# Adjacency and mixture-of-experts kernel on one core: z transposed through memory in 32 by 32 blocks, routing chain among the Q items, z's scaling one item later

## The chip, the cores and the metric

The kernel runs on one core of one Trainium2 chip. The metric is the device time in microseconds of one execution, lower is better. TensorE (PE in the profile) does the matmuls, VectorE (DVE) and ScalarE (ACT) the elementwise work, GpSimd (POOL) small statistics and one sum, and SyncE (SP) issues all transfers.

## The reference

```python
def _l0_gnn(x):                                  # on layernorm(x), x is (16, 512, 128)
    h = x @ fc_in_w.T + fc_in_b
    alph = sigmoid(alpha_train)[:, None]
    w_eff = w * clip(d, 0, 1) @ w.T
    for _ in range(8):                           # dt = 1/8
        f = alph * 0.5 * (adj @ h - h) + h @ w_eff - h + x
        h = h + dt * f
    return h

def _moe(tokens):                                # on layernorm(x), 8 experts, top 2
    probs = softmax(tokens @ router_w.T)
    rw, re = top_k(probs, 2); rw = rw / rw.sum(-1)
    out = tokens
    for e in range(8):
        out = out + combine[:, e:e + 1] * (gelu(tokens @ w1[e] + b1[e]) @ w2[e] + b2[e])
    return out

x = x + _l0_gnn(layernorm(x))
x = x + _moe(layernorm(x))
```

## The kernel before

The 16 batches are worked on in 8 groups of two (`GB = 2`). A group passes through two halves of a pipeline. In iteration `g`, the graph part of group `g` runs first and then the experts of group `g - 1`. Iteration 0 has no experts, iterations 1 to 6 are one loop body, and iteration 7 and the experts of group 7 are written out behind it. Every product is taken in three matmuls of a high and a low part (`mm3`, lines 1034 to 1036): ScalarE copies the high part (`high`, line 414), and VectorE subtracts it for the low part (`low`, line 605).

**Graph part.** The eight Euler steps are folded into a polynomial. TensorE multiplies the normalised input x0 with two powers of the nodes' matrix (`nodes_product(0)` to `(3)`, two for each of the two batches; their results become G, tile `GT`), then, in eight Q items of nine matmuls each, G by the features' powers `M` (line 1255); VectorE adds the bias to each item (line 957), and an item may not start before the sum of the one four back. Two stages of a Horner scheme with the nodes' matrix follow (`y1`, then `h8`), and the result is x1 (line 1000). Its statistics (line 609) go to GpSimd, which works out the inverse root in ten small operations (`inverse_root`, lines 366 to 387).

**Experts.** `experts(h, g, more)` runs 16 items for group `h`: item `i` is batch `i // 8`, expert `i % 8`. For an item TensorE does the up product (three matmuls of 512 columns), ScalarE the gelu (line 537), VectorE the scaling with the routing weight (line 902), ScalarE the high part, VectorE the low part, and TensorE, five items later (`LAG`), the down product (lines 1211 and 1218). From item 3 on an up product waits for the gelu of three items before. Among the items stand the steps for group `g`, which is one ahead: `scale_z` (z is x1 normalised; VectorE does batch 0 in two calls from item `Z_SCALE = 4` on, ScalarE batch 1 in four), then `transpose_z` on TensorE behind items 10 and 11 (`Z_ITEM`; four 128 by 128 blocks each, line 1168, into PSUM), its high part (`high_z`) and its low part (`low_z`), which together are `zT`. `logits` (line 1160) multiplies `zT` with the router's weights behind item 15.

**Tail of an iteration.** Behind the items TensorE still has five down products, with `nodes_product(0)` of group `g + 1` between them, then `nodes_product(1)`, the transposes of the output (line 1174), `nodes_product(2)`, and `nodes_product(3)` as the next iteration's first work. VectorE adds the output (`add_out`, line 890) and starts the routing chain.

**Routing.** `route_start` and the four parts of `route_on` are a chain of small VectorE operations (top 2 of 8, the weights by a tanh on ScalarE, `route_tanh`), at whose end `comb_out` holds the weights. SyncE stores them to memory (line 316) and loads them back replicated over the partitions (`replicate`, line 293), and ScalarE copies them for TensorE (`copy_comb`).

**x0's transpose** already goes through memory from group 2 on: SyncE stores x0 (`keep_x0`, line 299), reads it back with the 32 by 32 blocks in their transposed places (`blocks_of_x0`, line 307, runs of 128 bytes), and VectorE turns the inside of each block (`turn_x0`, line 662).

All orders are written out by hand, one list for each engine, and semaphores join them. SyncE's list matters here as well: it is one queue, in which a wait holds back all that stands behind it. In one iteration it is `expert_weights` (stores of the routing weights, `keep_x0`, then the replicating loads and `blocks_of_x0`), `next_x`, `store`.

## Time and profile before

| | us |
|---|---|
| median of 3 runs | 546.7 (546.55 to 547.36) |
| the profiled execution, its own time | 547.12 |
| its span, first to last instruction | 545.3 |
| TensorE busy / VectorE busy / ScalarE busy | 529.6 / 440.0 / 307.3 |
| mean granted TensorE clock | 0.995 |

The span is what the trace shows; 1.8 us of the profiled time lie around it. "Busy" of an engine is the time in which it had an instruction running; matmuls overlap, so the starts of matmuls tell more than their lengths. In a timeline, the number in brackets is how long the engine stood idle before the row, and what ended that.

### The profile page before, as it was taken

Reading aid. Unit: us, or ns where it says so; the run is one execution under the profiler, and the core shown is the slowest. Engines: PE = TensorE matmul, PEld = TensorE weight load, DVE = VectorE, ACT = ScalarE, POOL = GpSimd, SP = SyncE. Lnnn points to the kernel's source line nnn. Section 1 sums busy time; section 2 is a strip of 40 time slices with the busy share of each in tenths; the row PEclk is TensorE's granted clock in tenths of the full one; section 3 lists DMA queues with packets and bytes.
Section 4 is the critical chain, followed back from the end, with each engine's and each line's share of the span. In section 5 each row is a group of like instructions: output and inputs, shape, how many; then the busy total and the mean of one; then the engine's idle time right before and its main releaser. Section 6 shows DMA issues by size and latency. Waiting matters only on the chain.

```text
span 545.3 us, 9197 instructions
## 1 busy us (share of the span) xinstructions
PE 529.6 (97%) x2895; PEld 462.4 (85%) x2895; DVE 440.0 (81%) x1000; ACT 307.3 (56%) x553; POOL 97.1 (18%) x178
## 2 busy tenths in 40 slices
PE   5999999999999999999999999999999999999796
PEld 4787998997899888997899888998899788987585
DVE  6888677688877998689877998589877996489995
ACT  6324423458535893468535893469445882158584
POOL 1204013222040402122040402121030401031100
PEclk9999999999999999999999999999999999999999
DMA  4040010193006701292007601292008400260151
GB/s 129 2 115 1 0 41 0 53 264 112 20 22 175 248 0 38 65 269 92 19 22 196 227 0 38 74 272 80 19 22 225 159 12 27 56 242 14 41 193 40
DMA packets 57375, 49.45 MB, mean 91 GB/s; under 512 B 26774, under 2 KB 51980, under 8 KB 55436
## 3 DMA queue, kind: packets, MB, share of 16 engines
q1 hardware_dynamic: 57356, 49.22, 29.9%
q8 instruction: 9, 0.15, 0.1%
q14 instruction: 10, 0.08, 0.0%
HBM read 41.61 MB, written 7.60 MB: 90 GB/s over the span
## 4 chain that ended last, share of the span: by engine, by line
PE 70%; issue 14%; POOL 6%; DVE 5%; ACT 2%; DMA 1%; SPq 0%; POOLq 0%; DVEq 0%; ACTq 0%
PE bank L1034 18%; PE bank L1036 18%; PE bank L1035 17%; PE bank L1211 8%; PE bank L1218 4%; POOL rstd L385 2%; DVE work L902 1%; PE bank L1174 1%; DVE scs L605 1%; ACT work L537 1%; PE bank L1160 1%; POOL scr L393 1%; PE bank L1168 1%; DMA work<-in_adj_dram 1%; PE bank L1062 1%
## 5 line engine op out<-in xcount | busy, mean ns | idle before, releaser
L537 ACT ACTIVATE work<-bank,cols 128x512 f32<-128x512 f32 x128 | 87.9, 688 | 17.4 <-PE bank L1036 17.4
L605 DVE TENSOR_TENSOR scs<-work,scs 128x512 fp32r<-128x512 f32 x132 | 91.0, 690 | 1.9 <-ACT scs L414 0.5
L414 ACT ACTIVATE scs<-work 128x512 fp32r<-128x512 f32 x132 | 83.6, 634 | 8.7 <-DVE work L902 7.8
L1211 PE MATMUL bank<-scs,w2s 128*128 128x512 f32 x256 | 80.7, 396 | 0.0
L1034 PE MATMUL bank<-M,GT 128*128 128x384 f32 x192 | 64.3, 335 | 1.0 <-DVE GT L605 1.0
L1036 PE MATMUL bank<-M,GT 128*128 128x384 f32 x192 | 64.2, 335 | 0.0
L1035 PE MATMUL bank<-M,GT 128*128 128x384 f32 x192 | 64.2, 334 | 0.0
L902 DVE TENSOR_TENSOR work<-work,GT 128x512 f32<-128x512 f32 x90 | 61.4, 688 | 3.3 <-ACT work L537 1.9
L957 DVE TENSOR_TENSOR Q<-bank,bias 128x384 f32<-128x384 f32 x64 | 35.4, 553 | 31.9 <-PE bank L1036 31.0
L1211 PEld LDWEIGHTS bank<-scs,w2s 128*128 128x128 f32 x256 | 47.5, 188 | 10.3
L1034 PE MATMUL bank<-zT,w1s 128*128 128x512 f32 x128 | 53.7, 420 | 1.0
L1034 PE MATMUL bank<-LT,x0s 128*128 128x512 f32 x128 | 51.7, 404 | 0.0
L1036 PE MATMUL bank<-zT,w1s 128*128 128x512 f32 x128 | 50.8, 397 | 0.0
L1218 PE MATMUL bank<-scs,w2s 128*128 128x512 f32 x128 | 50.6, 396 | 0.0
L1035 PE MATMUL bank<-zT,w1s 128*128 128x512 f32 x128 | 50.6, 395 | 0.0
L1036 PE MATMUL bank<-LT,x0s 128*128 128x512 f32 x128 | 50.1, 392 | 0.0
L1035 PE MATMUL bank<-LT,x0s 128*128 128x512 f32 x128 | 49.8, 389 | 0.0
L393 POOL TENSOR_TENSOR scr<-Q,scr 128x1024 f32<-128x1024 f32 x8 | 19.2, 2400 | 171.8 <-DVE outs L890 169.5
L370 POOL TENSOR_TENSOR mv<-bn 128x8 f32<-128x8 f32 x16 | 4.8, 303 | 239.9 <-DVE bn L609 239.9
L414 ACT ACTIVATE GT<-bank 128x512 fp32r<-128x512 f32 x36 | 21.1, 594 | 44.9 <-PE bank L1036 42.3
L414 ACT ACTIVATE scs<-Q 128x512 fp32r<-128x512 f32 x16 | 10.1, 632 | 60.8 <-DVE Q L957 60.8
L1034 PEld LDWEIGHTS bank<-M,GT 128*128 128x128 f32 x192 | 36.0, 188 | 1.6 <-issue 1.3
(187 smaller groups left out, 1264.2 us busy)
## 6 DMA issues: line engine op xcount, KB each, us to landing
GT<-comb_rows SPq DMA_DIRECT2D x8, 1536.0 KB, 7.0
Q<-comb_rows SPq DMA_DIRECT2D x16, 512.0 KB, 6.8
GT<-comb_rows SPq DMA_DIRECT2D x7, 1024.0 KB, 5.6
xn<-in_x_dram SPq DMA_DIRECT2D x16, 256.0 KB, 7.9
out_dram<-outs SPq DMA_DIRECT2D x16, 256.0 KB, 2.3
GT<-comb_rows SPq DMA_DIRECT2D x7, 512.0 KB, 4.1
x_rows<-x SPq DMA_DIRECT2D x12, 256.0 KB, 2.6
x0q<-x_rows SPq DMA_DIRECT2D x24, 128.0 KB, 4.1
```

Source lines behind the costliest of these rows:

```text
L385: nc.gpsimd.tensor_tensor(rstd[:, n, :], ve[:, n, :], nhalf[:, :], ALU.pow).then_inc(ln_rstd[n], 1)
L393: nc.gpsimd.tensor_tensor(res, x1, z, ALU.add).then_inc(res_ready, 1)
L414: return nc.scalar.activation(dst, src, ACT.Copy)
L537: nc.scalar.activation(hid[:, i % 2, :], bank[UP_BANK[i % 3]][:, :], ACT.Gelu, bias=cols[:, B1_COL + e:B1_COL + e + 1]).then_inc(gelu_done, 1)
L605: return v.tensor_tensor(dst, src, hi.bitcast(FP32), ALU.subtract)
L902: v.tensor_tensor(scaled[:, i % 3, :], hid[:, i % 2, :], bank[REP_BANK[i % 2]][:, :] if by_pe else rep(i), ALU.mult).then_inc(sc_ready, 1)
L957: v.tensor_tensor(Q[:, :, t, b, :], src, bias[:, t], ALU.add).then_inc(q_ready, 1)
L1034: pe.matmul(dst, wh, xh, start=start, stop=False)
L1035: pe.matmul(dst, wh, xl, start=False, stop=False)
L1036: return pe.matmul(dst, wl, xh, start=False, stop=stop)
L1211: pe.matmul(bank[SUM_BANK[b]][:, :], w2s[:, k, e, :], scs[:, i % RING, 0, :], start=(e == 0 and k == 0), stop=False)
L1218: pe.matmul(bank[SUM_BANK[b]][:, :], w2s[:, 0, e, :], scs[:, i % RING, 1, :], start=False, stop=(e == E - 1)).then_inc(down_mm, 1)
```

## The change

z of the iterations with `more` (groups 1 to 6) is no longer transposed on TensorE. SyncE stores it to a new memory tensor `z_rows` in two transfers and reads it back in eight of 32 partitions each, 16 by 32 runs of 128 bytes, into `zq`; VectorE turns the blocks into `zt` behind the output's first sum, and the high and low parts of `zT` are taken from `zt`. Group 0 and group 7 still use TensorE, group 7 behind items 10 and 12. The logits move behind `nodes_product(2)` (in iteration 7 two steps later than before). The routing chain's start moves to VectorE's last place in the iteration; its four parts follow the first, second, fourth and fifth Q item of the next one. `route_tanh` and `copy_comb` move along on ScalarE. Half of the input's statistics stand behind the low part of G's fourth product. z's scaling starts at item 5. GpSimd's `variance` joins two sums in one operation. `lgT` now lies in the memory of `cc`. The scratch for dynamic transfers is 1024 instead of 4096.

```diff
         shift = sb("shift", [P, 2, T])
+        zq = sb("zq", [P, GB, N])
+        zt = sb("zt", [P, GB, N])
         zT = sb("zT", [P, 2, GB, N], F32R)
...
         rm = sb("rm", [P, 10, T])
-        lgT = sb("lgT", [P, T, R])
         cc = sb("cc", [P, T, 4, E])
+        lgT = cc[:, :, :, :].rearrange("p t k e -> p t (k e)")
         combT = sb("combT", [P, H], F32R)
...
         REP_BANK, REP_PE = [3, 7], 6
-        Z_SCALE, Z_ITEM = 4, 10
+        Z_SCALE, Z_AT = 5, [10, 12]
+        ROUTE_AT = [0, 1, 3, 4]
         UP_BANK, SUM_BANK = [4, 5, 6], [0, 1]
...
                                  blocks[j]).then_inc(x0q_in, 16)
+            def blocks_of_z(g):
+                for b in range(GB):
+                    sp.wait_ge(z_ready, GB * g + b + 1)
+                    sp.dma_start(z_rows[b].rearrange("(t p) c -> p t c", p=P), z[:, :, b, :]).then_inc(z_kept, 16)
+                sp.wait_ge(z_kept, 32 * g)
+                for b in range(GB):
+                    blocks = z_rows[b].rearrange("(i q) (j a) -> j q i a", q=32, a=32)
+                    for j in range(4):
+                        sp.dma_start(zq[32 * j:32 * (j + 1), b, :].rearrange("p (i a) -> p i a", a=32),
+                                     blocks[j]).then_inc(zq_in[b], 16)
...
                 next_x(g + 2)
+                blocks_of_z(g)
                 store(g - 1)
...
                 expert_weights(g - 1, g, g < GROUPS - 1)
+                if g < GROUPS - 1:
+                    blocks_of_z(g)
                 store(g - 1)
...
                 nc.gpsimd.tensor_tensor(mv[:, n, 1, :], mean_e, mean_o, ALU.subtract)
-                nc.gpsimd.tensor_tensor(mv[:, n, 2, :], bn[:, n, :, 2], bn[:, n, :, 5], ALU.add)
-                nc.gpsimd.tensor_tensor(mv[:, n, 0, :], mean_e, mean_o, ALU.add).then_inc(ln_sums[n], 1)
+                nc.gpsimd.tensor_tensor(mv[:, n, 0:3:2, :].rearrange("p k t -> p t k"), bn[:, n, :, 1:3],
+                                        bn[:, n, :, 4:6], ALU.add).then_inc(ln_sums[n], 1)
                 pool.wait_ge(ln_sums[n], 3 * g + 1)
...
-            def high_z(g, b, banks=ZT_BANK):
-                act.wait_ge(zt_mm, GB * g + b + 1)
+            def high_z(turn, b, banks=ZT_BANK):
+                act.wait_ge(zt_mm, GB * turn + b + 1)
                 high(zt_part(0, b), bank[banks[b]][:, :]).then_inc(zt_hi, 1)
+            def high_turned_z(g, b):
+                act.wait_ge(z_turned, GB * (g - 1) + b + 1)
+                high(zt_part(0, b), zt[:, b, :]).then_inc(zt_hi, 1)
...
                         scale_z(g, 1, i - Z_SCALE - 1)
-                    if i == Z_ITEM + 1 and g is not None:
-                        high_z(g, 0)
+                    if i - 1 in Z_AT and g is not None and not more:
+                        high_z(1, Z_AT.index(i - 1))
                     if i == ITEMS - 4:
                         copy_sum(h, 0)
-                    if i == Z_ITEM + 2 and g is not None:
-                        high_z(g, 1)
                 item_high(h, ITEMS - 1)
...
                 copy_sum(h, 1)
+                if more:
+                    for b in range(GB):
+                        high_turned_z(g, b)
                 if g is not None and not more:
...
                     high_gt(g, 3, 3)
+                    route_tanh(g - 1)
                 for p in range(2):
...
                     high(y2s[:, 0, 2 * p:2 * p + 2], Q[:, 2, 2 * p:2 * p + 2]).then_inc(y2_hi, 1)
-                    if p == 0 and not first:
+                    if p == 1 and not first:
                         copy_comb(g - 1)
...
                     for b in range(GB):
-                        high_z(g, b, ZT_FIRST)
+                        high_z(0, b, ZT_FIRST)
                     high_gt(g + 1, 2, 2)
-                    route_tanh(g)
                 else:
...
                     if not final:
-                        high_gt(g + 1, 0, 0)
-                        route_tanh(g)
-                        for k in range(1, 3):
+                        for k in range(3):
                             high_gt(g + 1, k, k)
...
+            def turn_z(g, b):
+                dve.wait_ge(zq_in[b], 64 * g)
+                v.transpose(zt[:, b, :], zq[:, b, :]).then_inc(z_turned, 1)
+            def low_turned_z(g, b):
+                dve.wait_ge(zt_hi, GB * g + b + 1)
+                low(zt_part(1, b), zt[:, b, :], zt_part(0, b)).then_inc(zt_lo, 1)
             def add_out(h, b):
...
                         scale_z(g, 0, i - Z_SCALE)
-                    if i in (Z_ITEM + 1, Z_ITEM + 2) and g is not None:
-                        low_z(g, i - Z_ITEM - 1)
+                    if i - 1 in Z_AT and g is not None and not more:
+                        low_z(g, Z_AT.index(i - 1))
                 item_low(h, ITEMS - 1)
                 add_out(h, 0)
-                if g is not None:
+                if g is not None and not more:
                     route_start(g)
...
                     for b in range(GB):
+                        turn_z(g, b)
+                    for b in range(GB):
                         low_turned(g + 1, b)
-                    route_on(g, 0)
+                    for b in range(GB):
+                        low_turned_z(g, b)
                     low_gt(g + 1, 0, 0)
...
                     low_gt(g + 1, 1, 1)
-                    route_on(g, 1)
                     low_gt(g + 1, 2, 2)
+                    route_start(g)
...
                 if not first and not final:
-                    for b in range(GB):
-                        norm_x_stats(g + 1, b)
+                    norm_x_stats(g + 1, 0)
                 if not first:
                     low_gt(g, 3, 3)
+                if not first and not final:
+                    norm_x_stats(g + 1, 1)
...
                     v.tensor_tensor(Q[:, :, t, b, :], src, bias[:, t], ALU.add).then_inc(q_ready, 1)
-                    if not first and i < 2:
-                        route_on(g - 1, 2 + i)
+                    if not first and i in ROUTE_AT:
+                        route_on(g - 1, ROUTE_AT.index(i))
                     if first and i in (1, 3):
...
                     route_start(g)
-                    route_on(g, 0)
-                    route_on(g, 1)
                 else:
...
                                   start=False, stop=(e == E - 1)).then_inc(down_mm, 1)
-                    if s in (Z_ITEM, Z_ITEM + 1) and g is not None:
-                        transpose_z(g, s - Z_ITEM)
+                    if s in Z_AT and g is not None and not more:
+                        transpose_z(g, Z_AT.index(s))
                     if s == ITEMS - 1:
                         transpose_out(h, 0)
-                        if g is not None:
-                            logits(g)
+                    if s == ITEMS + 1 and g is not None and not more:
+                        logits(g)
                     if s >= ITEMS and more:
...
                     nodes_product(2)
+                    logits(g)
...
-    nc = _bacc.Bacc("TRN2", target_bir_lowering=False, num_devices=1, dynamic_dma_scratch_size=4096)
+    nc = _bacc.Bacc("TRN2", target_bir_lowering=False, num_devices=1, dynamic_dma_scratch_size=1024)
     arrays, args = {}, []
```

TensorE, loop body: up product 10, down product 5, then up product 11 (`bank<-ident,scr` is a transpose of z). Before:

```order
L1034 MATMUL bank<-zT,w1s 128x512
L1035 MATMUL bank<-zT,w1s 128x512
L1036 MATMUL bank<-zT,w1s 128x512
L1211 MATMUL bank<-scs,w2s 128x512 x2
L1218 MATMUL bank<-scs,w2s 128x512
L1168 MATMUL bank<-ident,scr 128x128 x4
L1192 REGISTER_ALU
L1034 MATMUL bank<-zT,w1s 128x512
L1035 MATMUL bank<-zT,w1s 128x512
```

Now:

```order
L1067 MATMUL bank<-zT,w1s 128x512
L1068 MATMUL bank<-zT,w1s 128x512
L1069 MATMUL bank<-zT,w1s 128x512
L1244 MATMUL bank<-scs,w2s 128x512 x2
L1251 MATMUL bank<-scs,w2s 128x512
L1225 REGISTER_ALU
L1067 MATMUL bank<-zT,w1s 128x512
```

The four transposes between a down product and the next up product are gone; the next set, an item later, goes the same way.

TensorE, loop body, from behind the last up product. `bank<-ident,yT` is the output's transpose, `zT,rts` and `zT_next,rts` are the logits. Before:

```order
L1211 MATMUL bank<-scs,w2s 128x512 x2
L1218 MATMUL bank<-scs,w2s 128x512
L1174 MATMUL bank<-ident,yT 128x128 x4
L1160 MATMUL bank<-zT,rts 128x256 x4
L1160 MATMUL bank<-zT_next,rts 128x256 x4
L1211 MATMUL bank<-scs,w2s 128x512 x2
L1218 MATMUL bank<-scs,w2s 128x512
```

Now, the same place and the end of the loop body:

```order
L1244 MATMUL bank<-scs,w2s 128x512 x2
L1251 MATMUL bank<-scs,w2s 128x512
L1207 MATMUL bank<-ident,yT 128x128 x4
L1244 MATMUL bank<-scs,w2s 128x512 x2
L1251 MATMUL bank<-scs,w2s 128x512
...
L1067 MATMUL bank<-LT,x0s 128x512
L1068 MATMUL bank<-LT,x0s 128x512
L1069 MATMUL bank<-LT,x0s 128x512
L1193 MATMUL bank<-zT,rts 128x256 x4
L1193 MATMUL bank<-zT_next,rts 128x256 x4
L1320 REGISTER_ALU
L1320 COMPARE_AND_BRANCH
```

The logits left the place behind the output's first transpose; they now stand behind `nodes_product(2)`, as the last work of the loop body.

VectorE, loop body, behind the last item, from the output's first sum. Before:

```order
L887 ISA
L889 ISA
L890 TENSOR_TENSOR outs<-bank,scr 128x512
L843 STREAM_TRANSPOSE lgT<-bank 128x256
L845 TENSOR_REDUCE rt<-lgT 128x64
L846 TENSOR_REDUCE rm<-rt 128x8
L847 TENSOR_TENSOR rt<-rt,rm 128x64
L605 TENSOR_TENSOR GT<-x0t,GT 128x512 x2
L853 SCALAR_TENSOR_TENSOR rt<-rt,rank 128x64
```

Now, from the same sum on to the start of the routing chain (`cc<-bank`):

```order
L918 ISA
L921 TENSOR_TENSOR outs<-bank,scr 128x512
L911 STREAM_TRANSPOSE zt<-zq 128x512 x2
L628 TENSOR_TENSOR GT<-x0t,GT 128x512 x2
L628 TENSOR_TENSOR zT<-zt,zT 128x512
L628 TENSOR_TENSOR zT_next<-zt,zT_next 128x512
L628 TENSOR_TENSOR GT<-bank,GT 128x512
L921 TENSOR_TENSOR outs<-bank,scr 128x512
L628 TENSOR_TENSOR GT<-bank,GT 128x512
L628 TENSOR_TENSOR GT<-bank,GT 128x512
L866 STREAM_TRANSPOSE cc<-bank 128x256
```

The routing chain's start gives way to two block transposes of z; z's two low parts come behind x0's, and the routing chain starts behind the third low part of G.

## Rows read from the trace of the kernel before

**Rows 1.** the page's section 1 (engine: busy us, share of the span, instructions).
```profile
PE 529.6 (97%) x2895; PEld 462.4 (85%) x2895; DVE 440.0 (81%) x1000; ACT 307.3 (56%) x553; POOL 97.1 (18%) x178
```

**Rows 2.** TensorE's waits (waiter <- releaser: total us, times, longest).
```profile
PEld bank L1034 <- ACT work L537: 7.3, 17, 0.5
```

**Rows 3.** timeline of TensorE, group 1 (start us, us, engine, line, operation, count).
```profile
131.05 0.60 PE L1168 MATMUL bank<-ident,scr 128*128 128x128 f32 x4
131.41 0.48 PE L1034 MATMUL bank<-zT,w1s 128*128 128x512 f32 x1
131.72 0.40 PE L1035 MATMUL bank<-zT,w1s 128*128 128x512 f32 x1
```

**Rows 4.** the same timeline, around items 9 and 10.
```profile
127.40 0.40 PE L1218 MATMUL bank<-scs,w2s 128*128 128x512 f32 x1
127.79 0.50 PE L1034 MATMUL bank<-zT,w1s 128*128 128x512 f32 x1
...
129.06 0.39 PE L1218 MATMUL bank<-scs,w2s 128*128 128x512 f32 x1
129.56 0.50 PE L1034 MATMUL bank<-zT,w1s 128*128 128x512 f32 x1
```

**Rows 5.** timelines of VectorE and ScalarE, z's scaling in group 1.
```profile
126.67 0.61 DVE L619 TENSOR_SCALAR scr<-Q,mv,rstd 128x128 f32<-128x128 f32 x2 [1.23 <-POOL shift L387]
...
131.65 0.48 ACT L519 ACTIVATE scr<-Q,shift,rstd 128x128 f32<-128x128 f32 x1
```

**Rows 6.** timelines of TensorE and ScalarE, start of group 1's feature product.
```profile
95.84 0.34 PE L1036 MATMUL bank<-M,GT 128*128 128x384 f32 x1
97.15 0.44 PE L1034 MATMUL bank<-M,GT 128*128 128x384 f32 x1 [0.97 <-DVE GT L605]
...
93.23 0.21 ACT L503 ACTIVATE rm<-rm 128x8 f32<-128x8 f32 x1 [3.24 <-DVE rm L859]
...
95.72 0.58 ACT L414 ACTIVATE GT<-bank 128x512 fp32r<-128x512 f32 x1
```

**Rows 7.** timelines of VectorE and TensorE, group 2.
```profile
159.31 0.22 DVE L874 TENSOR_TENSOR cc<-rt 128x64 f32<-128x64 f32 x1
...
163.51 0.56 DVE L957 TENSOR_TENSOR Q<-bank,bias 128x384 f32<-128x384 f32 x1 [1.00 <-PE bank L1036]
...
176.56 1.31 DVE L662 STREAM_TRANSPOSE x0t<-x0q 128x512 f32<-128x512 f32 x2 [0.25 <-DMA x0q<-x_rows]
...
181.10 1.31 DVE L902 TENSOR_TENSOR work<-work,GT 128x512 f32<-128x512 f32 x2 [0.31 <-ACT work L537]
...
182.59 0.39 PE L1036 MATMUL bank<-zT,w1s 128*128 128x512 f32 x1
183.08 0.50 PE L1034 MATMUL bank<-zT,w1s 128*128 128x512 f32 x1
```

**Rows 8.** timeline of SyncE's queue, group 2 (start and length of issuing).
```profile
160.88 1.72 SPq L316 DMA_DIRECT2D comb_rows<-comb_out  x4
166.59 0.94 SPq L299 DMA_DIRECT2D x_rows<-x  x2
...
169.93 3.37 SPq L307 DMA_DIRECT2D x0q<-x_rows  x4
```

**Rows 9.** timelines of ScalarE and TensorE, tail of group 1.
```profile
147.02 0.60 ACT L414 ACTIVATE yT<-bank 128x512 f32<-128x512 f32 x1 [3.46 <-PE bank L1218]
...
139.51 0.72 PE L1160 MATMUL bank<-zT,rts 128*128 128x256 f32 x4
...
140.54 0.63 PE L1211 MATMUL bank<-scs,w2s 128*128 128x512 f32 x2
...
155.49 0.33 PE L1034 MATMUL bank<-M,GT 128*128 128x384 f32 x1
```

**Rows 10.** timeline of TensorE; windows view (length, busy us by engine, granted clock, DMA, GB/s).
```profile
515.48 0.73 PE L1182 MATMUL bank<-combT,pick 128*128 128x256 f32 x4 [2.74 <-ACT combT L414]
...
515.50:519.80 4.30, 4.30 (x16) 3.51 (x17) 3.67 (x7) 2.59 (x5) 2.39 (x1) 0.61 0.31 81
```

More of the change, by code:

```diff
@@ L42, with build @@
 RING = 6
-def build(nc, x, adj, alpha, w, d, fc_w, fc_b, router_w, w1, b1, w2, b2, comb_rows, x0_rows, out):
+def build(nc, x, adj, alpha, w, d, fc_w, fc_b, router_w, w1, b1, w2, b2, comb_rows, x0_rows, z_rows, out):
     B, N, D = x.shape
@@ L191, in build @@
         zt_moved = sem("zt_moved")
+        z_kept, zq_in, z_turned = sem("z_kept"), [sem(f"zq_in{b}") for b in range(GB)], sem("z_turned")
         lg_mm, rt_own, rt_pre, rt_tanh, comb_ready = (sem(n) for n in ("lg_mm", "rt_own", "rt_pre", "rt_tanh", "comb_ready"))
@@ L1311 @@
     args.append(nc.dram_tensor("x0_rows", (2, N, shape[2]), _mybir.dt.float32, kind="Internal").ap())
+    args.append(nc.dram_tensor("z_rows", (2, N, shape[2]), _mybir.dt.float32, kind="Internal").ap())
     args.append(nc.dram_tensor("out_0_dram", shape, _mybir.dt.float32, kind="ExternalOutput").ap())
```

## The prediction

> **What bounds the kernel now.** I read the page's busy times first. TensorE is busy for 97% of the span, VectorE for 81%, ScalarE for 56% [rows 1]. A busy share alone proves little, so the waits come next: TensorE's weight loads waited 7.3 us for ScalarE's gelu, in 17 pieces [rows 2], and from the first group to the last its matmuls stood only once for anything else, 1.0 us in group 1 [rows 6]. So the end is set by TensorE's own list of matmuls. What shortens that list shortens the kernel, as long as no new wait comes up in it. The timeline of TensorE shows this: in the item stage a matmul of 512 columns starts 0.23 us after the one before, six of them make an item of 1.40 us, and where a start comes later than that, a wait for gelu stands behind it [rows 3, 4].
>
> **The transposes of z leave TensorE** in groups 1 to 6 (group 0 and group 7 keep theirs). Four blocks start at 131.05 and the next matmul at 131.41, 0.36 us on; the one after it comes 0.31 instead of 0.23 us later [rows 3]. So a set costs 0.36 + 0.08 = 0.44 us, there are two sets in a group, and 12 x 0.44 = 5.3 us go. The Trainium skill speaks against the change: "VectorE: DVE Perf Modes", section "Rules for kernel authors", says to transpose a full 128x128 block on TensorE if a result in PSUM will do, and it does here. That rule looks at the instruction and not at which engine is full; the same page's table gives 390 ns for a block, by which 48 blocks would be worth 18.7 us, where the row bears out 0.09 us for a block in a row of four, and the row decides.
>
> **z's scaling one item later, and a shorter chain on GpSimd.** In group 1, VectorE comes to z's scaling 1.23 us before GpSimd has the inverse root, and stands with two items' work behind it [rows 5]. ScalarE's share of the scaling waits for the same value, its gelus come late, and TensorE starts two items late: 127.79 instead of 127.63, and 129.56 instead of 129.29 [rows 4]. That is 0.16 + 0.27 us, and 0.1 us more each time for the slower start of the second matmul, like the 0.08 us of [rows 3]: 0.63 us. The same pattern stands in groups 3 and 7 of the timeline, not in 2, 4, 5 and 6. One item more of VectorE's work is two operations of 0.6 us, 1.2 us, which covers the 1.23 us; GpSimd also saves one small operation. I take all of it: 3 x 0.63 = 1.9 us. The least is half of it, the most is this.
>
> **Routing among the Q items.** In group 1 TensorE stands 1.14 us at its 19th feature matmul, for the low part of G's fourth product, and by the same slower start about 0.1 us more [rows 6]. Behind this is ScalarE: the tanh waited 3.24 us for the routing chain, and only then, 2.5 us on, comes the copy that is wanted [rows 6]. In the changed kernel tanh stands behind that copy, and half of the statistics too. The 18 starts up to 95.84, at 0.174 us, put the end of the fourth product at 92.9, ScalarE then copies at once, VectorE has its low part near 94.3, and TensorE wants it at 96.0: 1.25 us go, once. At worst nothing of it goes. In the later groups nothing waits there before, and I cost the routing operations at nothing on TensorE: VectorE has up to 1.0 us free between two Q items, and TensorE only waits for the sum of the item four back. If that cover went, each late item would cost its lateness.
>
> **What this delays.** The chain's last part now follows the fifth Q item's sum, not the second's. In group 2 that sum starts at 163.51 and the next operation could start 0.48 us on, at 163.99 (that is the step after the second's sum); from the start of the last part at 159.31 to SyncE's first store at 160.88 it took 1.57 us, and the four stores took 1.72 us to issue [rows 7, 8]. So they now end at 163.99 + 1.57 + 1.72 = 167.28. Behind them in SyncE's queue is the store of x0's rows, which began at 166.59: it slips by 0.69 us, and so do the block loads behind it. VectorE already waits for those before its block transpose [rows 7]. Its 4.5 us from there to the first item's scaling have one pause of 0.31 us, just before it [rows 7], so the scaling slips by 0.38 us. The third gelu stands behind that scaling, and TensorE's item 5 waits for the gelu already: it starts at 183.08, 0.26 us late [rows 7]. So 0.38 us comes back to TensorE in each of the six groups with x0 blocks, **+2.3 us**. At least it is nothing (if SyncE finishes sooner), at most the whole 0.69, 4.1 us.
>
> **z's way through memory** is ten transfers, two block transposes on VectorE, two copies on ScalarE and two subtractions on VectorE, which come out of the items (there they were too, reading PSUM) into the tail. z is complete near 132.1, as before: ScalarE's last piece started at 131.65 [rows 5], one item later now but without the wait. Storing x0's rows and having them took 169.93 - 166.59 = 3.3 us [rows 8], so the block loads start near 135.4. x0's four, with the same bytes in the same runs, took 176.56 - 169.93 = 6.6 us to the transpose [rows 7, 8]; eight of half the size I take for the same: 142.0. That is when VectorE has finished the items. Then a transpose (0.6), x0's two low parts (1.2) and z's two (1.2), with 0.2 between: 145.2, if ScalarE is there. ScalarE copies the second sum first; that was at 147.02 [rows 9] and is now 1.14 us (group 1's own 0.88 + 0.64 - 0.38) and 1.03 us (the logits moved away, 139.51 to 140.54) earlier, 144.9; z's two copies follow, and z's low parts end near 147.2. TensorE reaches the moved logits at 155.49 - 1.14 - 1.03 - 12 x 0.23 = 150.6 [rows 9]. So 3.4 us are to spare, and the whole way costs nothing. What is queued behind that wait on TensorE is the fourth nodes product and all Q items, so if the cover goes, it costs one to one. The Trainium skill's "DMA: Bandwidth & Descriptors", section "Specifications", has transfers under 512 B read, modify and write, and z's runs are 128 B; it gives no price. x0's runs are the same 128 B, and their rows are what I use.
>
> **End.** Before the last items TensorE waits 2.74 us for the last weights, and then a stretch of 4.3 us has a mean granted clock of 0.61 [rows 10]: it ran mostly at 1.2 and not 2.4 GHz. VectorE's chain to those weights runs without pause, and was held by the scaling's wait in group 7. It comes up to 1.2 us sooner (its wait, as in [rows 5]), of which 0.6 is counted above; the later logits (two items on) still come before VectorE asks. I take 0.4 us more, 0 to 0.6. The low clock stays.
>
> **Sum**, against the profiled execution's 547.1: -5.3 - 1.9 - 1.25 - 0.4 + 2.3 = -6.55, so 540.6. That execution is 0.4 us above the median of 546.7; against the median it is **540.2 us**, 1.2% less. A measurement of this kernel tells about 0.2% (1.1 us) from no change.
>
> **Rivals.**
> - *z comes late and TensorE waits at the logits* (slower). The whole gain is 1.1 us for each of the six groups, so it turns when z's low parts end at 151.7, that is when the blocks are there at 148.5: 13.1 us after the first issue instead of 6.6. If eight transfers took twice as long as x0's four (13.3 us, 148.7), TensorE would wait until 151.9, 1.3 us a group, 7.8 us in all: 548.0. For it: SyncE issues eight where it issued four, issuing x0's four took 3.37 us [rows 8], and the rule on small transfers. Against it: the bytes are equal, and nothing else moves then. 0.08.
> - *The item stage is not TensorE's.* If the transposes lie in the shadow of ScalarE and VectorE, the 5.3 us stay: 545.5. For it: gelu ends are close to TensorE's starts in every group. Against it: VectorE's item is 1.2 us and TensorE's is 1.40. 0.07.
> - *x0's delay is swallowed*: no +2.3, so 537.9. SyncE's queue might be free sooner. 0.17.
> - *The change doesn't do what it says*: z's scaling waits as before, and group 1's stall stays, 543.3. 0.06.
> - *The end's wait gets short enough that the clock stays up*: 4.3 x (1 - 0.61) = 1.7 us [rows 10], 538.5. Against it: the wait barely shrinks. 0.03.
>
> The forecast itself has 0.57, and 0.02 is for what I don't see. **The range**: the low end has x0's delay at nothing and the end's 0.6 (537.7), and goes 0.7 on, as far as a part of the clock's case would take it, 537.0; the high end has 4.1 us for x0's delay, nothing from group 1's stall and half of the scaling's: 544.2, which takes in the fourth rival. Outside are z late and the item stage. Faster by over 0.2% is every case but z late and part of what I don't see and of the second rival, whose 545.5 is at the limit: 0.87; within 0.2%, 0.05; slower, 0.08.
>
> **What would show it.** TensorE's list without transposes of z between 120 and 500; no weight load of item 9 or 10 that waits for gelu; no wait at the 19th feature matmul; item 5 late by about 0.6 instead of 0.26 us; the transpose of x0 waiting about 0.9 us; the logits without a wait, and z's transpose done before 144. Wrong would be: a wait for VectorE's z before the logits, or a group that is less than 0.5 us shorter (starts of two comb stores apart, 60.8 us before).

## The result and the profile after

The changed kernel takes **537.7 us** (median of 5 runs, 537.13 to 538.87) where the kernel before takes 546.55 us (5 runs, 545.9 to 547.36). The ratio is 0.9831, with a 95% interval of 0.9814 to 0.9848. The forecast was 540.2 us with a range of 537.0 to 544.2. The profiled execution took 537.13 us with a span of 535.3 us, the shortest of the five. The medians are 8.85 us apart and the two profiled spans 10.0 us; executions of one kernel lie up to 1.7 us apart here, and up to 2.6 us among 20 of the kernel before.

The page's busy times and TensorE's largest waits for the other engines in the item stage, with the wait of VectorE for x0's blocks (waiter <- releaser: total us, times, longest):

```profile
PE 521.2 (97%) x2847; PEld 456.9 (85%) x2847; DVE 433.3 (81%) x1012; ACT 309.2 (58%) x553; POOL 95.3 (18%) x162
```
```profile
PEld bank L1067 <- ACT work L561: 3.7, 7, 0.6
DVE x0t L685 <- DMA x0q<-x_rows: 3.2, 6, 0.7
```

TensorE has 48 matmuls fewer, its share of busy time is the same 97% [rows 1], and the waits for gelu fell from 7.3 us in 17 pieces to 3.7 in 7 [rows 2]. It still sets the end, with a shorter list. Around items 9 and 10 of group 1 every start is now where 0.23 us puts it [rows 4], and VectorE comes to the scaling of z without a wait:

```profile
127.18 0.39 PE L1251 MATMUL bank<-scs,w2s 128*128 128x512 f32 x1
127.41 0.40 PE L1067 MATMUL bank<-zT,w1s 128*128 128x512 f32 x1
...
128.57 0.40 PE L1251 MATMUL bank<-scs,w2s 128*128 128x512 f32 x1
128.81 0.40 PE L1067 MATMUL bank<-zT,w1s 128*128 128x512 f32 x1
```

At the start of group 1 the 19th feature matmul starts at 95.63, 0.18 us behind the one before it (the first was at 92.50). ScalarE's tanh still waits 3.16 us for the routing chain, but with nothing behind it that TensorE wants [rows 6]. Timelines of TensorE and ScalarE in group 1:

```profile
95.45 0.33 PE L1069 MATMUL bank<-M,GT 128*128 128x384 f32 x1
95.63 0.33 PE L1067 MATMUL bank<-M,GT 128*128 128x384 f32 x1
...
96.43 0.21 ACT L527 ACTIVATE rm<-rm 128x8 f32<-128x8 f32 x1 [3.16 <-DVE rm L882]
```

z's way through memory in group 1, on SyncE's queue, VectorE, ScalarE and TensorE in turn. VectorE finds the blocks there, and the operation behind its last low part starts at 145.30, 3.4 us before the logits at 148.69:

```profile
132.73 4.04 SPq L323 DMA_DIRECT2D zq<-z_rows  x8
139.80 1.29 DVE L911 STREAM_TRANSPOSE zt<-zq 128x512 f32<-128x512 f32 x2
142.94 0.60 ACT L433 ACTIVATE yT<-bank 128x512 f32<-128x512 f32 x1 [3.34 <-PE bank L1251]
143.96 0.62 ACT L433 ACTIVATE zT_next<-zt 128x512 fp32r<-128x512 f32 x1
144.70 0.69 DVE L628 TENSOR_TENSOR zT_next<-zt,zT_next 128x512 fp32r<-128x512 f32 x1
148.69 0.64 PE L1193 MATMUL bank<-zT,rts 128*128 128x256 f32 x4
```

x0's way in group 2, the counterpart of [rows 7] and [rows 8]. The four stores of the routing weights start at 162.43, the rows of x0 at 164.25, and VectorE waits 0.50 us for the blocks. Item 5 starts late by 0.27 us, as it did before:

```profile
162.43 1.72 SPq L332 DMA_DIRECT2D comb_rows<-comb_out  x4
164.25 0.94 SPq L303 DMA_DIRECT2D x_rows<-x  x2
165.80 0.36 SPq L297 DMA_DIRECT2D GT<-comb_rows  x1
167.64 2.74 SPq L311 DMA_DIRECT2D x0q<-x_rows  x4
...
173.69 1.30 DVE L685 STREAM_TRANSPOSE x0t<-x0q 128x512 f32<-128x512 f32 x2 [0.50 <-DMA x0q<-x_rows]
...
177.98 1.33 DVE L933 TENSOR_TENSOR work<-work,GT 128x512 f32<-128x512 f32 x2
...
179.97 0.50 PE L1067 MATMUL bank<-zT,w1s 128*128 128x512 f32 x1
```

**Where the 10.0 us of span went.** From group 1's first feature matmul to group 2's it is 59.87 us instead of 62.62, so 2.75 less. From group 2's first store of routing weights to group 7's it is 299.15 instead of 304.27, 5.12 less (59.9 a group; before 60.7, and 61.4 in group 3, where z's scaling was late). The setup was 0.38 us shorter. Its length varies: the second pair of input loads starts at 25.80 to 26.62 us in the 11 profiles of the changed kernel and its variants, and at 26.56 to 27.44 in the three with the kernel before's setup. How much of it is the change's is open. The remaining 1.75 us lie in group 7 (0.63, z's scaling) and at the end (1.1). There the wait for the last weights is 2.08 instead of 2.74 us, and in the profiled execution the clock stays up behind it, unlike in [rows 10]. From that wait's end to the last instruction it is 29.33 instead of 29.82 us. With x0's blocks first (below) the same wait of 2.08 us was followed by a falling clock and 29.81 us, so the clock was worth 0.5 us. The 1.7 us that the prediction gave it did not come, as TensorE now reaches the other engines' results sooner: it waits 0.34 us for VectorE at 509.79.

```profile
505.97 0.73 PE L1215 MATMUL bank<-combT,pick 128*128 128x256 f32 x4 [2.08 <-ACT combT L433]
...
506.00:510.00 4.00, 3.66 (x18) 2.65 (x19) 3.37 (x6) 2.54 (x5) 2.40 (x1) 1.00 0.29 78
```

### The profile page after: what moved, and what is told of

Read it like the earlier page. It is cut to its first block, busy times and chain, and to the rows that moved or that the text cites. A ratio compares the mean times of both kernels' runs of the same rounds, so it can differ in the third digit from the quotient of the medians.

```text
span 535.3 us, 9155 instructions
## 1 busy us (share of the span) xinstructions
PE 521.2 (97%) x2847; PEld 456.9 (85%) x2847; DVE 433.3 (81%) x1012; ACT 309.2 (58%) x553; POOL 95.3 (18%) x162
## 4 chain that ended last, share of the span: by engine, by line
PE 87%; DVE 6%; ACT 3%; issue 2%; DMA 1%; POOL 1%; SPq 0%; DVEq 0%; ACTq 0%; POOLq 0%
PE bank L1067 23%; PE bank L1069 23%; PE bank L1068 22%; PE bank L1244 10%; PE bank L1251 5%; DVE work L933 2%; ACT work L561 2%; DVE scs L628 1%; PE bank L1193 1%; PE bank L1207 1%; DMA work<-in_adj_dram 1%; PE bank L1095 1%; PE bank L1248 1%; DVE scr L642 1%; ACT scs L433 1%
## 5 line engine op out<-in xcount | busy, mean ns | idle before, releaser
L1067 PE MATMUL bank<-zT,w1s 128*128 128x512 f32 x128 | 51.6, 403 | 0.7
L1069 PE MATMUL bank<-zT,w1s 128*128 128x512 f32 x128 | 50.3, 393 | 0.0
L1068 PE MATMUL bank<-zT,w1s 128*128 128x512 f32 x128 | 50.1, 391 | 0.0
L628 DVE TENSOR_TENSOR GT<-bank,GT 128x512 fp32r<-128x512 f32 x36 | 24.4, 685 | 18.8 <-ACT GT L433 18.8
```

The lines of the kernel that those rows point to most:

```text
L628: return v.tensor_tensor(dst, src, hi.bitcast(FP32), ALU.subtract)
L1067: pe.matmul(dst, wh, xh, start=start, stop=False)
L1068: pe.matmul(dst, wh, xl, start=False, stop=False)
L1069: return pe.matmul(dst, wl, xh, start=False, stop=stop)
```

## The experiments

Twelve kernels were run, each on one chip together with the kernel before, whose times its ratio uses; the chip was not the same for all twelve. Spans and groups come from their profiles; a group is the distance from its first store of routing weights to the next group's. "Late" is the time by which a start comes after the place that 0.23 us a matmul puts it.

### The parts put back: z's transposes, z's scaling

**z back on TensorE.** The changed kernel with z transposed by TensorE in groups 1 to 6 and without z's way through memory: its two stores of rows, its eight block loads, VectorE's block transposes and the copies behind them are all gone.

```
-                blocks_of_z(g)
...
-                    if s in Z_AT and g is not None and not more:
+                    if s in Z_AT and g is not None:
                         transpose_z(g, Z_AT.index(s))
```

> The changed kernel with one part undone: in groups 1 to 6 TensorE transposes z again, behind items 10 and 12, and nothing of z goes through memory. Theory A (TensorE's list of matmuls sets the end, a set of four blocks costs it 0.44 us): every group is 0.88 us longer than the changed kernel's 59.87 us, 60.75 us, and the whole is 5.3 us longer, near 543.0 us. Theory B (the item stage belongs to VectorE and ScalarE, and what counts is that z's high and low parts left it): the groups get longer by waits for gelu or for low parts in the items, and not by 0.44 us at the transposes. Theory C (the transposes lay in the others' shadow): 538 us.

Measured: 543.11 us, ratio 0.9923 (0.9906 to 0.9939), span 541.3. A group takes 60.8 us instead of 59.87, 0.9 us more, and no wait is there that the changed kernel doesn't have. TensorE loses to the transposes what their rows say, 0.44 us a set, and nothing of it lies in another engine's shadow.

**z's scaling back by one item.**

```
-        Z_SCALE, Z_AT = 5, [10, 12]
+        Z_SCALE, Z_AT = 4, [10, 12]
```

> The changed kernel with z's scaling back at item 4. Theory A (the scaling's place covers the inverse root's delay): VectorE waits for the root again, near 0.6 us since GpSimd has one operation less, and items 9 and 10 start late again in some groups: 1 to 2 us longer, 539 to 540 us. Theory B (GpSimd's shorter chain did it, or the transposes' departure leaves enough room): no difference within 0.3 us, 537.7 us.

Measured: 542.67 us, ratio 0.9918 (0.9902 to 0.9935), span 540.5: 5 us, more than either theory had. Groups 1 to 6 take 60.33, 60.93, 60.30, 60.93, 59.77 and 59.81 us; 3.0 us are lost there, and 2.4 in the last group and the end, where the wait for the last weights is back at 2.74 us and the clock falls (it stayed up in the profile after). In groups 2 and 4 VectorE waits 1.24 us for the inverse root and three items are late instead of two; in groups 1 and 3 it waits 0.64 us and one item is late. That the third item is late because no transposes stand ahead of it any more is argued from its place and not shown. Timelines of VectorE and TensorE in group 2 (the third late item is at 189.79):

```profile
185.19 0.60 DVE L642 TENSOR_SCALAR scr<-Q,mv,rstd 128x128 f32<-128x128 f32 x2 [1.24 <-POOL shift L406]
...
186.31 0.50 PE L1067 MATMUL bank<-zT,w1s 128*128 128x512 f32 x1
...
188.07 0.50 PE L1067 MATMUL bank<-zT,w1s 128*128 128x512 f32 x1
...
189.79 0.50 PE L1067 MATMUL bank<-zT,w1s 128*128 128x512 f32 x1
```

### The parts alone, on the kernel before

**Routing among the Q items alone.**

```
+        ROUTE_AT = [0, 1, 3, 4]
...
-                    if not first and i < 2:
-                        route_on(g - 1, 2 + i)
+                    if not first and i in ROUTE_AT:
+                        route_on(g - 1, ROUTE_AT.index(i))
```

> The kernel before with the move of the routing chain alone: GpSimd's and VectorE's parts of it among the Q items, the tanh behind the copies, half of the statistics behind G's fourth low part. z's transposes stay on TensorE and z's scaling stays where it was. Theory A: it is worth the stall of group 1 at the 19th feature matmul, 1.25 us, and nothing else: 545.3 us for 546.6, a ratio of 0.9977; the later store of x0's rows is swallowed as in the whole change. Theory B: with TensorE's transposes in place the later x0 costs what was predicted, 0.38 us in six groups: 547.6 us, a ratio of 1.002.

Measured: 547.24 us, ratio 1.0005 (0.9992 to 1.0018); the profiled execution was the slowest of ten, span 546.6. Group 1's stall is gone, and item 5 is late by 0.27 us as before, so Theory A is right on both. Its time is not: 0.9977 lies outside the interval, and the measured time is nearer Theory B's, for a reason that neither has. z's scaling now makes items late in groups 1 to 5 and 7 of the profile (group 4 by twice as much), where before it did in 1, 3 and 7: the gain is given back. Timelines of GpSimd and VectorE in group 2, of the kernel before and then of this one:

```profile
180.87 0.21 POOL L370 TENSOR_TENSOR mv<-bn 128x8 f32<-128x8 f32 x1 [20.39 <-DVE bn L609]
181.03 0.21 POOL L371 TENSOR_TENSOR mv<-bn 128x8 f32<-128x8 f32 x1
181.20 0.66 POOL L372 TENSOR_TENSOR mv<-bn 128x8 f32<-128x8 f32 x1
...
187.44 0.60 DVE L619 TENSOR_SCALAR scr<-Q,mv,rstd 128x128 f32<-128x128 f32 x2 [0.63 <-POOL shift L387]
```
```profile
179.99 1.30 DVE L901 TENSOR_TENSOR work<-work,GT 128x512 f32<-128x512 f32 x2 [0.24 <-ACT work L538]
179.99 0.75 POOL L372 TENSOR_TENSOR mv<-bn 128x8 f32<-128x8 f32 x1
180.70 0.66 POOL L373 TENSOR_TENSOR mv<-bn 128x8 f32<-128x8 f32 x1
...
186.94 0.60 DVE L618 TENSOR_SCALAR scr<-Q,mv,rstd 128x128 f32<-128x128 f32 x2 [1.23 <-POOL shift L388]
```

GpSimd's second operation takes 0.21 us where VectorE still pauses (its first item began at 181.10, after 0.31 us [rows 7]) and 0.75 us where VectorE's first item starts with it. GpSimd's chain to the shift is 7.1 us long instead of 6.5, and VectorE waits 0.6 us more at z's scaling. In group 1 of the kernel before, a late one, that second operation had 0.68 us too.

The same holds in the other groups with x0 blocks, of both kernels: where VectorE pauses for 0.30 or 0.31 us before its first item, it later waits 0.63 us at z's scaling; where it pauses for 0.24 us or less, it waits 1.23 us or more. The pause is short where VectorE waited long for x0's blocks ahead of it (0.39 to 0.80 us, against 0.32 at most where it is whole). So by these rows a later x0 is paid at z's scaling and not at item 5, and the later place of z's scaling covers that in the changed kernel. No run moved x0 alone on the kernel before, so this is argued.

**z's scaling one item later alone.**

```
-        Z_SCALE, Z_ITEM = 4, 10
+        Z_SCALE, Z_ITEM = 5, 10
```

> The kernel before with z's scaling one item later and nothing else. Theory A: this part is worth the late items behind z's scaling where they stood before, in groups 1, 3 and 7, three times 0.63 us, 1.9 us as in the prediction: 544.8 us, a ratio of 0.9965; the run with the routing moved alone had those late items in every group from 1 on, so the part is worth more only beside the other one. Theory B: the run of the whole change without this part lost 5 us, and it is worth that wherever it is made: 542 us, a ratio of 0.991.

Measured: 544.57 us, ratio 0.9945 (0.9931 to 0.996), span 543.9 against 545.3. The late items of groups 1, 3 and 7 are gone (groups 1 and 3 are 0.6 us shorter, the other four agree to 0.1), and the end's wait is 2.24 instead of 2.74 us: 1.9 + 0.5 = 2.4 us by the trace, 0.9956. That is Theory A with the term for the end, which the expectation had left out; the spans are only 1.4 us apart because this execution's setup was 0.87 us longer. Theory B's 5 us are far outside. The part is worth 2.4 to 3 us alone and 5 beside the others.

### How much x0's way has to spare

**The last part of the routing one Q item later, and two.**

```
-        ROUTE_AT = [0, 1, 3, 4]
+        ROUTE_AT = [0, 1, 3, 5]
```

> The changed kernel with the routing chain's last part behind the sixth Q item instead of the fifth, so that the weights come 1.56 us later. Theory A (the delay goes from the stores of the weights over x0's stores and block loads to the block transpose, from there to the first item's scaling and to TensorE's item 5, and what little slack there is was used up by the change): VectorE waits near 2.0 us for x0's blocks instead of 0.5, item 5 starts 1.5 us later, 1.4 us a group for six groups, 546 us. Theory B (the block loads have slack, as they met fewer other transfers in the changed kernel and so ended sooner): less than 0.3 us a group, under 539.5 us.

> The same with the last part behind the seventh Q item, 3.1 us later than in the changed kernel. Theory A: 3.0 us a group, 555 to 556 us. Theory B: 538 to 545 us, the more so as the replicating load of the first weights is then late as well.

Measured: 544.92 us, ratio 0.9957 (0.994 to 0.9973), and with [0, 1, 3, 6] 556.47 us, ratio 1.0176 (1.0153 to 1.0199). In the first, item 5 is late by 0.8 us in place of 0.27, and in groups 1 to 5 TensorE also waits 0.3 to 1.1 us at the experts' first product, for the sum of x1, because VectorE stands at x0's transpose ahead of it. In the second that wait is 1.4 to 2.2 us, in all six groups. The times are near Theory A's. So x0 is wanted, and a delay of one Q item costs 1.3% of the time. That the 0.7 us of the change cost nothing needed another reason.

**The replicating load right ahead of x0's blocks, and behind them.** The first load behind x0's rows replicates routing weights, into the memory of the tile `GT` ("the load that replicates G" in the expectations). In the first of two kernels SyncE waits for x0's rows before it issues that load; in the second it issues the blocks first.

```
+                if more:
+                    sp.wait_ge(x0_kept, 32 * g)
+                    sp.wait_ge(x0t_lo, GB * (g + 1))
                 if g is not None:
                     replicate(h, 0, 2, 0, 0)
```
```
+                if more:
+                    blocks_of_x0(g + 1)
...
                 if g is not None:
                     replicate(h, 0, 2, 0, 0)
-                    if more:
-                        blocks_of_x0(g + 1)
```

> The changed kernel, with SyncE waiting for x0's rows (and for the buffer of its blocks) before it issues the first load that replicates G, instead of behind it. So that load leaves right before x0's four block loads, as it did more nearly in the kernel before (1.01 us ahead of the first of them there, 1.84 us in the changed kernel). Theory A: x0's four block loads became faster with the change (6.05 instead of 6.63 us from the first issue to the turn) because the replicating load no longer stands right ahead of them; that swallowed the 0.7 us by which SyncE came later. Here they take 6.6 us or more again, VectorE's block transpose of x0 comes 0.5 us later or more, 0.3 to 0.5 us of it reaches TensorE at item 5 of each of six groups: about +2 to +3 us, near 540 us. Theory B: the time of the block loads has nothing to do with what is issued ahead of them, and x0's way has slack: no difference, 537.7 us.

> The changed kernel, with x0's four block loads issued ahead of the first load that replicates G instead of behind it. The run before this one with that load right in front of the blocks had the blocks' issue at 3.92 us instead of 2.74 and x0 0.5 to 0.6 us later. Theory A: what lets x0 in by the time it is wanted is the distance to the load ahead; with nothing ahead the blocks are there at least as early, VectorE's 0.50 us wait before x0's transpose shrinks, and TensorE gains nothing by it, since its late item 5 hangs on the first gelu of the group and not on x0: 537.7 us, a ratio of 0.983, item 5 still 0.27 us late. Theory B: item 5 hangs on x0's blocks, and its lateness shrinks with them: up to 0.38 us in six groups, 535.4 us.

Measured: 548.56 us, ratio 1.0037 (1.0021 to 1.0052), and 537.59 us, ratio 0.9827 (0.9796 to 0.9859). SyncE's queue and VectorE in group 2 of the first:

```profile
171.09 0.36 SPq L297 DMA_DIRECT2D GT<-comb_rows  x1
171.55 3.92 SPq L311 DMA_DIRECT2D x0q<-x_rows  x4
...
178.69 1.31 DVE L688 STREAM_TRANSPOSE x0t<-x0q 128x512 f32<-128x512 f32 x2 [2.25 <-DMA x0q<-x_rows]
```

and of the second, with TensorE's item 5:

```profile
167.73 2.16 SPq L311 DMA_DIRECT2D x0q<-x_rows  x4
...
173.24 1.30 DVE L685 STREAM_TRANSPOSE x0t<-x0q 128x512 f32<-128x512 f32 x2
...
179.59 0.39 PE L1069 MATMUL bank<-zT,w1s 128*128 128x512 f32 x1
180.10 0.50 PE L1067 MATMUL bank<-zT,w1s 128*128 128x512 f32 x1
```

With the kernel before, whose replicating load left at 168.92, these make a series (group 2 of each):

| replicating load ahead of x0's first block load by | SyncE issues the four in | first issue to VectorE's transpose | item 5 late by |
|---|---|---|---|
| 0.46 us (first kernel) | 3.92 us | 7.14 us | 0.83 us |
| 1.01 us (kernel before) | 3.37 us | 6.63 us | 0.26 us |
| 1.84 us (changed kernel) | 2.74 us | 6.05 us | 0.27 us |
| none ahead (second kernel) | 2.16 us | at most 5.51 us, no wait | 0.28 us |

The blocks come later the closer the load stands ahead of them. In the other groups the same times are 7.1 to 8.6 us, 6.4 to 7.0, 6.0 to 6.5 and 5.5 to 6.2 at most. Farther than 1.84 us the distance gains little: with the last part of the routing one Q item later the load stands 2.3 us ahead, and the blocks take 5.8 to 6.6 us. The Trainium skill, "DMA: Bandwidth & Descriptors", section "Queues, rings and completion order", has SyncE's DMAs share one ring on each of the same 16 engines, where descriptors are consumed in order; the series agrees with it.

Theory A has the cause right in both. Its price for the first kernel is not: it expected 2 to 3 us more than the changed kernel, and it was 10.9. TensorE also waits 0.7 to 2.2 us for x1's sum in groups 1 to 5, behind VectorE's wait for x0, and item 5 is late by 0.8 us. In the second kernel x0 is there without a wait, and item 5 is late all the same. In the changed kernel item 5 does not hang on x0.

### How much z's way has to spare

The first store of the results moves ahead of z's block loads (the counts of the stores behind it follow).

```
+                sp.wait_ge(out_add, 1 + GB * h + 1)
+                sp.dma_start(of_group(out_v, h, 0), outs[:, 0, :, :]).then_inc(out_stored, 16)
                 for b in range(GB):
```

> The changed kernel, with the block loads of z issued behind the first store of the results instead of ahead of it, about 7 us later (near 140 in place of 132.7 in group 1). Theory A: z's way has 3.4 us to spare, read as the time between the end of z's second low part (145.3) and the moved logits (148.7). A delay of 7 us less those 3.4 us is what TensorE waits at the logits, if nothing else moves: but VectorE's transpose was at 139.80 behind the items and now comes near 147, so its two low parts end near 149.2 to 152; TensorE waits 0.5 to 3 us in each of six groups: 541 to 555 us, and the wait stands at the logits. Theory B: z's values are wanted much later than that, or the block loads take less than the 7.1 us between issue and use: no difference.

Measured: 543.44 us, ratio 0.9947 (0.993 to 0.9964). In group 1:

```profile
140.31 4.71 SPq L325 DMA_DIRECT2D zq<-z_rows  x8
...
146.63 0.71 DVE L913 STREAM_TRANSPOSE zt<-zq 128x512 f32<-128x512 f32 x1 [1.38 <-DMA zq<-z_rows]
...
149.77 0.74 PE L1195 MATMUL bank<-zT,rts 128*128 128x256 f32 x4 [1.04 <-DVE zT_next L630]
```

The loads start 7.58 us later, and TensorE stands 0.9 to 1.2 us at the logits in every group: Theory A, at its low end. VectorE now waits for the blocks, so their time shows: 6.3 us from the first issue to the last transpose (6.6 was taken from x0). The loads had 6.4 us to spare (7.58 - 1.2), not 3.4: the 3.4 us are the slack of VectorE's low parts, which stand behind ScalarE's copy of the sum.

### Item 5, and a faster version

**ScalarE's third gelu first.**

```
-                    if i >= 1:
+                    if i == 2 and g is not None:
+                        item_high(h, 0)
+                    if i >= 2 or (i == 1 and g is None):
                         item_high(h, i - 1)
```

> The changed kernel, with ScalarE doing the gelu of item 2 before item 0's second copy (the one that needs VectorE's scaling of item 0), in all groups but the first. Theory A: TensorE's item 5 is late by 0.27 us, and the matmul behind it by 0.11, in six groups because the third gelu stands in ScalarE's queue behind a copy that waits for VectorE's first scaling. With the gelu ahead of that copy the 0.38 us goes: six times, 2.3 us, so about 535.4 us. Theory B: ScalarE has no room, so the copy that is now a gelu later makes a second product late instead, 0.2 to 0.4 us a group: 537 to 538 us, no difference, with TensorE's wait at another item.

Measured: 539.31 us, ratio 0.9868 (0.9846 to 0.989). Item 5 is on time, but VectorE waits 0.72 us for item 0's copy, stays 0.64 us behind, and behind z's scaling a weight load waits 0.31 us for gelu and one two items on 0.49 us (the second reaches the matmuls as 0.22 us, and each slow start costs another 0.1). A group takes 60.08 us, and the wait at the end is 3.02 instead of 2.08 us: Theory B, and a little worse.

**VectorE's third scaling first as well**, and the same with z's scaling one item later still (`Z_SCALE` 6).

```
-                    if i >= 1:
+                    if i == 2 and g is not None:
+                        item_low(h, 0)
+                    if i >= 2 or (i == 1 and g is None):
                         item_low(h, i - 1)
```

> The changed kernel, with the gelu of item 2 ahead of item 0's copy on ScalarE (as in the run with that alone) and VectorE scaling item 2 before it takes the low parts of items 0 and 1. The run with ScalarE's part alone took item 5's 0.27 us away and put 0.22 and 0.31 us at two later items instead, because VectorE waited 0.72 us for item 0's copy, and stayed 0.64 us behind until z's scaling. Theory A: with VectorE scaling item 2 in that wait, it is 0.5 us further on, the later lateness goes, and a group takes 59.5 us instead of 59.87: about 535.5 us, a ratio near 0.979. Theory B: ScalarE's own 1.2 us an item keeps it behind wherever VectorE is: 538.5 to 539.5 us, as with ScalarE's part alone.

> As the run before, with z's scaling one item later still (behind items 6 and 7 of VectorE, 7 to 10 of ScalarE). Theory A: another 0.19 us ahead for VectorE at z's scaling, so that no gelu is late behind it; z is complete 1.4 us later and its block loads start 1.4 us later, which the 6.4 us that the block loads had to spare (7.58 us later cost 1.2 us) hold without a wait: 59.5 us a group, about 535.5 us. Theory B: no lateness was left after the run before, and the last group, where z still goes over TensorE and its scaling is now right ahead of the transposes, pays up to 1 us: 0 to 1 us above the run before.

Measured: 535.54 us, ratio 0.9788 (0.9762 to 0.9814), and 535.34 us, ratio 0.9786 (0.976 to 0.9811). VectorE's items in group 2 of the first of these two:

```profile
177.29 1.31 DVE L935 TENSOR_TENSOR work<-work,GT 128x512 f32<-128x512 f32 x2
178.80 0.71 DVE L935 TENSOR_TENSOR work<-work,GT 128x512 f32<-128x512 f32 x1 [0.20 <-ACT work L561]
179.43 1.28 DVE L630 TENSOR_TENSOR scs<-work,scs 128x512 fp32r<-128x512 f32 x2
```

VectorE's wait of 0.72 us is down to 0.20, no item of TensorE is late, and groups take 59.57 us. Theory A is right, to 0.1 us. The second adds nothing measurable (a group 59.5 us), and its time fits both of its theories: no lateness was left. Both beat the changed kernel: its twin of the same chip, with x0's blocks first, ran 537.12 to 538.26 us, and these 535.04 to 535.88 and 534.96 to 535.76.

## Why the prediction was right, and where it was not

- **TensorE bounds, and the transposes of z are worth 5.3 us.** Right: 0.88 us a group by the transposes' own rows, 0.89 in the profile after, and 0.9 when they were put back. The prediction was right to go by the row and not by the 18.7 us that it worked out from a single block's price.
- **z's scaling, 3 x 0.63 = 1.9 us.** Right against the kernel before, and shown by the run with this part alone. The prediction did not see that the other parts need it. With the routing moved the late items come in six groups instead of three, and with the transposes gone as well they are three items in groups 2 and 4. What told groups 1 and 3 of the trace of before from 2, 4, 5 and 6 was VectorE's pause before its first item, 0.17 us or none against 0.30 or 0.31. It was not the three groups themselves that were special.
- **Group 1's stall, 1.25 us.** Right, once.
- **x0's delay, +2.3 us.** This is the step that failed, and it makes up nearly all of the 2.5 us between the forecast of 540.2 and the measured 537.7. "It slips by 0.69 us, and so do the block loads behind it" held: the rows slipped by 0.78 us against the group's first matmul (11.10 to 11.88), the first block load by 0.83 (14.44 to 15.27). But the 6.6 us from there to the transpose were taken as fixed, and they fell to 6.05, since the replicating load kept its place (13.43 us behind the group's first matmul in both profiles) while the blocks slipped away from it. The transpose slipped by 0.25 us, and VectorE's pause of 0.31 us, counted as a cover for 0.31 of 0.69, covered all of it: the first item's scaling stands 25.61 us behind the group's first matmul in both profiles. The case "x0's delay is swallowed" had 537.9 us and came true at 537.7, for a reason it did not name: SyncE was not free sooner. That the time lies inside the stated range, 0.7 us above its low end, is owed to the room left for this case.
- **z's way costs nothing, with 3.4 us to spare.** The cost was right, and the 3.4 us too, as the distance from VectorE's low parts to the logits. Both of its ends came 1.9 us earlier than predicted (145.3 for 147.2, 148.69 for 150.6): the prediction took off neither the stall of 1.25 us that group 1 loses nor the setup's 0.38, and it added 0.38 us for x0. As this moved both ends alike, the distance was right. The slack of the transfers themselves was larger, 6.4 us.
- **The end, 0.4 us, and the low clock stays.** The wait shrank by 0.66 us instead of 0.4. The clock stayed up in the profiled execution. The mean over the span is 1.000 in two of the five executions (spans 535.3 and 535.8 us) and 0.995 to 0.997 in the other three (535.9 to 537.0), so that rival came partly true. Its price did not: 0.5 us, not 1.7.

By the profiled executions: 5.3 + 1.9 + 1.25 for the three parts, 1.1 for the end, 0.4 in the setup, nothing for x0, 10.0 us. By the medians it is 8.85 us, which is what the prediction's terms make without x0's; that they agree this closely is luck, given the scatter of the executions. No run has z through memory alone on the kernel before, and none has GpSimd's shorter chain by itself.

## What to carry to other kernels

Where one engine is busy for 97% of the span, work taken off it is worth its own rows, but check each added wait against the engines' queues, since parts of a change cover for one another: here the routing's move alone gained nothing measurable, and z's scaling one item later was worth 2.4 to 3 us alone and 5 in company, though only 3.0 of these 5 lie in the groups. When a transfer slips, ask what it slips away from in the queue; the time of a transfer is not a constant. And when one late item hangs on two engines that wait for each other, reorder both or neither.

## What was not expected of the hardware

- **The time of a transfer of small runs depends on what was issued ahead of it.** 512 KB in runs of 128 B took from at most 5.5 us to 7.1 us in group 2, by the series above, and up to 8.6 us in group 1 of the kernel with the load right ahead. SyncE's issuing of the four loads took 2.15 to 4.34 us over all groups of these kernels.
- **The first operations of GpSimd's chain take 0.21 us or 0.64 to 0.75 us (once 1.18)**, the longer times where VectorE runs an operation with two SBUF inputs, as in the rows of GpSimd above. The Trainium skill, "SBUF — State Buffer", section "SBUF: two separate sides", has such a pair of operations block each other for a whole instruction; these rows agree. No run here moved GpSimd's chain by itself, so that this alone makes the difference between late and punctual groups was argued from the rows and not shown.
- **Behind a wait of about 2 us TensorE's clock falls in one execution and not in another.** With the same 2.08 us of waiting at the end, the profile after kept a granted clock of 1.00, and the kernel with x0's blocks first started its matmuls 0.43 us apart for the next 3 us (granted clock 0.53), the pace of 1.2 GHz, where 2.4 GHz gives 0.23. With ScalarE's third gelu first the clock stayed at 1.00 even behind 3.02 us. The length of the wait does not decide it inside one execution either. With the routing two items later the slow pace came behind waits of 2.23 us (group 2, granted clock 0.65 in the next 3.0 us) and 1.92 us (group 4, 0.63), and not behind 2.05 us (group 1) and 1.89 us (group 3), both 1.00. What decides stays open. TensorE in groups 1 and 4 of that kernel:

```profile
118.75 0.50 PE L1067 MATMUL bank<-zT,w1s 128*128 128x512 f32 x1 [2.05 <-DVE Q L1035]
...
119.56 0.40 PE L1067 MATMUL bank<-zT,w1s 128*128 128x512 f32 x1
119.79 0.39 PE L1068 MATMUL bank<-zT,w1s 128*128 128x512 f32 x1
...
308.33 0.50 PE L1067 MATMUL bank<-zT,w1s 128*128 128x512 f32 x1 [1.92 <-DVE Q L1035]
...
309.52 0.63 PE L1068 MATMUL bank<-zT,w1s 128*128 128x512 f32 x1
309.94 0.63 PE L1069 MATMUL bank<-zT,w1s 128*128 128x512 f32 x1
```
